# Softmax denominators in attention: GpSimd chains three heads over four key tiles, VectorE reduces the fourth head

## What is computed

```python
c6 = silu(c) @ Wc + bc
sh_msa, sc_msa, g_msa, sh_mlp, sc_mlp, g_mlp = jnp.split(c6, 6, axis=-1)
xm = _modulate(_ln(x), sh_msa, sc_msa)
q = (xm @ Wq + bq).reshape(B, S, NH, DH)
k = (xm @ Wk + bk).reshape(B, S, NH, DH)
v = (xm @ Wv + bv).reshape(B, S, NH, DH)
q = q / DH
w = jnp.einsum('bqhc,bkhc->bhqk', q, k)
w = jax.nn.softmax(w, axis=-1)
y = jnp.einsum('bhqk,bkhc->bqhc', w, v).reshape(B, S, H)
x = x + g_msa[:, None, :] * (y @ Wo + bo)
xm2 = _modulate(_ln(x), sh_mlp, sc_mlp)
h = jax.nn.gelu(xm2 @ W1 + b1, approximate=False)
x = x + g_mlp[:, None, :] * (h @ W2 + b2)
```

## Time and profile before

| | us |
|---|---|
| median of 3 runs | 2990.31 |
| lowest, highest | 2989.18, 2995.33 |
| the profiled execution | 2994.97 |
| its span, first to last instruction | 2993.0 |
| attention in it, first maximum to last sum | about 340 to 2102 |

### The profile page before, as it was taken

One profiled execution on the slowest core, in us unless ns is written; L12 is line 12 of the kernel. 1 busy time (PEld: TensorE's weight loads), 2 busy tenths in 40 slices (PEclk: granted clock), 3 DMA queues, 4 the chain that ended last, 5 costly groups with the idle time before them and its releaser, 6 DMA issues. The chain is left out here.

```text
span 2993.0 us, 40747 instructions
## 1 busy us (share of the span) xinstructions
PE 2886.8 (96%) x14713; PEld 1821.9 (61%) x14713; DVE 2092.1 (70%) x3415; ACT 1343.0 (45%) x2535; POOL 1969.7 (66%) x981
## 2 busy tenths in 40 slices
PE   7999999999999999999999999999699999999998
PEld 5777555455555555555555555553487787777777
DVE  5444687777777777787787777773757757766764
ACT  2222156566666666666666666666111111111111
POOL 1000079889898899898899899887454554545453
PEclk9999789999999999999999999999799999999999
DMA  6444822423414314314323224302201101101000
GB/s 225 176 172 168 204 58 62 95 59 71 103 42 99 88 34 97 86 44 97 79 65 86 68 65 96 77 20 100 88 15 43 42 1 43 43 9 34 29 15 15
DMA packets 152767, 225.19 MB, mean 75 GB/s; under 512 B 31804, under 2 KB 48760, under 8 KB 152568
## 3 DMA queue, kind: packets, MB, share of 16 engines
q1 hardware_dynamic: 123036, 204.81, 25.5%
q10 hardware_dynamic: 29532, 17.79, 2.2%
HBM read 162.30 MB, written 58.97 MB: 74 GB/s over the span
## 5 line engine op out<-in xcount | busy, mean ns | idle before, releaser
L828 DVE TENSOR_REDUCE part_max<-m_bank 128x1 f32<-128x512 f32 x2048 | 1252.4, 680 | 324.7 <-PE m_bank L918 324.6
L809 ACT ACTIVATE probs<-s_bank 128x512 f32<-128x512 f32 x2048 | 1038.7, 625 | 276.8 <-PE s_bank L932 272.8
L932 PE MATMUL s_bank<-qs,ks 97*128 97x512 f32 x2048 | 853.1, 418 | 2.5 <-ACT probs L809 2.4
L721 POOL TENSOR_TENSOR low_sum<-probs 128x1024 f32<-128x1024 f32 x248 | 599.1, 2426 | 188.8 <-ACT probs L809 188.8
L736 POOL TENSOR_TENSOR high_sum<-high_sum,probs 128x1024 f32<-128x1024 f32 x256 | 608.5, 2377 | 45.2 <-ACT probs L809 9.5
L932 PEld LDWEIGHTS s_bank<-qs,ks 97*128 97x128 f32 x2048 | 388.8, 190 | 344.4 <-issue 215.3
L942 PE MATMUL y_bank<-probs,vs 128*32 128x512 f32 x4096 | 504.3, 611 | 0.0
L1308 ACT ACTIVATE h<-up_bank,vecs 128x512 f32<-128x512 f32 x128 | 88.2, 689 | 635.4 <-PE up_bank L1333 635.4
L729 POOL TENSOR_TENSOR high_sum<-probs 128x1024 f32<-128x1024 f32 x128 | 307.7, 2404 | 12.8 <-ACT probs L809 12.8
L942 PEld LDWEIGHTS y_bank<-probs,vs 128*32 128x32 f32 x4096 | 108.3, 110 | 248.6 <-issue 139.1
L918 PE MATMUL m_bank<-space_parts,late_parts 96*128 96x512 f32 x512 | 214.3, 422 | 14.8 <-DVE part_max L828 14.2
(11 more groups left out here) (140 smaller groups left out, 3828.0 us busy)
## 6 DMA issues: line engine op xcount, KB each, us to landing
qs<-q_parts SPq DMA_DIRECT2D x96, 256.0 KB, 5.7
ks<-k_parts SPq DMA_DIRECT2D x96, 256.0 KB, 4.8
q_parts<-qk_out SPq DMA_DIRECT2D x32, 512.0 KB, 3.4
k_parts<-qk_out SPq DMA_DIRECT2D x32, 512.0 KB, 3.7
xb<-in_x SPq DMA_DIRECT2D x12, 1024.0 KB, 7.5
space_parts<-q_parts SPq DMA_DIRECT2D x48, 256.0 KB, 5.0
space_parts<-k_parts SPq DMA_DIRECT2D x48, 256.0 KB, 4.7
late_parts<-k_parts SPq DMA_DIRECT2D x48, 256.0 KB, 4.6
```

The lines of the kernel that those rows point to most:

```text
L721: pool.tensor_tensor(low_sum[:, (2 * c + half) % 4, :, :], probs[:, first % RING, hs, :], probs[:, (first + 1) % RING, hs, :], ALU.add).th ...
L809: act.activation(probs[:, tile % RING, h, :], s_bank[(HPG * tile + h) % 3][:, :], ACT.Exp).then_inc(p_done, 1)
L828: v.tensor_reduce(part_max[:, i % 2, hs, c:c + 1], m_bank[ring.bank["max", i, n]][:, :], AX.X, ALU.max).then_inc(m_taken, 1)
L932: pe.matmul(s_bank[n % 3][:, :], ks[:, h, t * P:(t + 1) * P], qs[i % 2][:, h, :], start=True, stop=True).then_inc(s_done, 1)
```

## The change

- GpSimd no longer makes separate pair sums. For each quad it runs one chain of three additions over **three** heads at once (128x1536) into `chain_sum`. In the last four quads the chain has two heads.
- DVE sums the **fourth** head: `quad` is a `tensor_reduce` over the four key tiles, in two halves of 256 columns. Each half reads 128x1024 values from `probs`, the four tiles innermost, so that consecutive elements lie 8 KB or 16 KB apart in a partition, and writes 128x256. The halves stand between the maxima, two for each quad. In the last four quads DVE sums two heads (`last_quad`), 512 columns at a time.
- All four heads of a quad are then one slot of `chain_sum`, so PE has 4 matmuls for every quad.
- `probs` holds 6 key tiles instead of 5.
- The multiplication of `y_buf` by `inv` goes from DVE to GpSimd, ahead of the chain of the iteration's fourth quad. DVE keeps it only for the last iteration. ACT issues the store of `y` one key tile later.

```diff
-RING = 5
+RING = 6
+CHAIN = HPG - 1
...
-        probs = sb("probs", [P, RING, HPG, TOK])
...
+        probs = sb("probs", [P, RING // 2, 2, HPG, TOK])
...
+        chain_sum = sb("chain_sum", [P, 2, HPG, TOK])
...
+            def chain(c, r):
+                hs = chain_heads(c)
                 pool.wait_ge(p_done, HPG * (4 * c + r) + hs.stop)
...
+                pool.tensor_tensor(chain_sum[:, c % 2, hs, :], first, prob(4 * c + r, hs), ALU.add).then_inc(chain_step, 1)
+
+            def normalise(i):
+                pool.wait_ge(y_taken, i + 1)
+                pool.wait_ge(inv_in, 16 * (i + 1))
+                pool.tensor_tensor(y_buf[:, :], y_buf[:, :], inv[:, :], ALU.mult).then_inc(y_normed, 1)
 
             for c in range(N_QUADS):
...
+                if c >= QPI and c % QPI == QPI - 1:
+                    normalise(c // QPI - 1)
+                for r in (1, 2, 3):
+                    chain(c, r)
...
+            def four_tiles(c, h, cols):
+                first = 4 * c % RING // 2
+                pairs = probs[:, first:first + 2] if first < 2 else probs[:, 0:3:2]
+                return pairs[:, :, :, h, cols].rearrange("p a b n -> p n a b")
+
+            def quad(c, half):
+                if half == 0:
+                    v.wait_ge(p_done, HPG * (4 * c + 4))
+                    if c >= 2:
+                        v.wait_ge(d_done, c - 1)
+                cols = slice(half * TOK // 2, (half + 1) * TOK // 2)
+                v.tensor_reduce(chain_sum[:, c % 2, CHAIN, cols], four_tiles(c, CHAIN, cols), AX.XY, ALU.add).then_inc(quad_ready, 1)
...
+                    if i and n in (14, 17):
+                        quad(QPI * i - 1, (14, 17).index(n))
+                    if n in (30, 33):
+                        quad(QPI * i, (30, 33).index(n))
...
-                    if i and n == NORMALISE_AT:
-                        normalise(i - 1, (inv_in, 16 * i))
+                    if n in (46, 49):
+                        quad(QPI * i + 1, (46, 49).index(n))
+                    if n == 61:
+                        quad(QPI * i + 2, 0)
...
                 as_row(i + 1)
+                quad(QPI * i + 2, 1)
```

More of the change, by code:

```diff
@@ L616, in attend, with prob, chain_heads @@
         wo_in, next_in = sem("wo_in"), sem("next_in")
-        def low_heads(c):
-            return slice(0, 2) if c % 2 == 0 else slice(2, 4)
-        def high_heads(c):
-            return slice(2, 4) if c % 2 == 0 else slice(0, 2)
-        def lows(c, n):
-            return (low_ready, 2 * c + n) if c < LAST_QUAD else (last_low_ready, 2 * (c - LAST_QUAD) + n)
-        def low_slot_free(c, half):
-            return c - 1 + half if c % 2 == 0 else c - 1
+        def prob(tile, heads):
+            slot = tile % RING
+            return probs[:, slot // 2, slot % 2, heads, :]
+        def chain_heads(c):
+            return slice(0, CHAIN if c < LAST_QUAD else 2)
         block = ctx.enter_context(nc.Block())
@@ L713, in _ @@
             pool.memset(ks[STACK:STACK + 1, :, :].bitcast(F32), 1.0).then_inc(ones_row, 1)
-            def low(c, half):
-                first = 4 * c + 2 * half
-                hs = low_heads(c)
-                if c >= 2:
-                    pool.wait_ge(d_done, low_slot_free(c, half))
-                pool.wait_ge(p_done, HPG * (first + 1) + hs.stop)
-                pool.tensor_tensor(low_sum[:, (2 * c + half) % 4, :, :], probs[:, first % RING, hs, :],
-                                   probs[:, (first + 1) % RING, hs, :], ALU.add).then_inc(low_ready, 1)
@@ L808, in _ @@
                             slot_free(tile - RING)
-                        act.activation(probs[:, tile % RING, h, :], s_bank[(HPG * tile + h) % 3][:, :], ACT.Exp).then_inc(p_done, 1)
+                        if tile >= RING:
+                            reduced_free(tile - RING, h)
+                        act.activation(prob(tile, h), s_bank[(HPG * tile + h) % 3][:, :], ACT.Exp).then_inc(p_done, 1)
                     if i:
@@ L891, in _ @@
                         maximum(i + 2, n)
+            for half in range(2):
+                quad(LAST_QUAD - 1, half)
             for q in range(QPI):
-                for half in range(2):
-                    last_low(LAST_QUAD + q, half)
+                for h in range(2, HPG):
+                    last_quad(LAST_QUAD + q, h)
                 if q == 1:
                     invert_small(N_IT - 2)
-                if q == 2:
-                    normalise(N_IT - 2, (inv_in, 16 * (N_IT - 1)))
             for n in range(4):
                 invert_last(n)
-            normalise(N_IT - 1, (inv_ready, 4))
+            normalise_last()
         @block.tensor
@@ L941, in times_v @@
                 for h in range(HPG):
-                    last = pe.matmul(y_bank[h * DH:(h + 1) * DH, :], vs[:, t, h * DH:(h + 1) * DH], probs[:, tile % RING, h, :],
+                    last = pe.matmul(y_bank[h * DH:(h + 1) * DH, :], vs[:, t, h * DH:(h + 1) * DH], prob(tile, h),
                                      start=(t == 0), stop=(t == NKT - 1))
@@ L954, in sums @@
                 first, final = c <= LAST_QUAD, c < LAST_QUAD or c == N_QUADS - 1
[L955 to L970 removed]
+                pe.wait_ge(chain_step, 3 * c + 3)
+                if c < LAST_QUAD:
+                    pe.wait_ge(quad_ready, 2 * (c + 1))
+                else:
+                    pe.wait_ge(last_ready, 2 * (c - LAST_QUAD + 1))
+                for h in range(HPG):
+                    last = add_up(c, h, chain_sum[:, c % 2, h, :], first, final)
                 last.then_inc(d_done, 1)
```

85 lines of the change are left out of this document (31 added, 54 removed).

## The result

| | before | after |
|---|---|---|
| median, us | 2989.74 | 3242.95 |
| lowest, highest | 2988.69, 2995.33 | 3241.48, 3245.19 |
| runs | 4 | 4 |
| the profiled execution, us (span) | 2994.97 (2993.0) | 3241.48 (3239.6) |

The changed kernel takes 1.084 times as long, 95% interval 1.082 to 1.086: 253 us more. I had predicted 175 us more, 3165 us, with a range up to 3240. The direction and most of the mechanism held; the time lies 3 us outside the range and 78 us above the forecast. The step that failed is X, the time by which one half delays the maxima behind it.

What follows compares the result with a forecast made beforehand. PE was taken to set the pace of attention. Terms of -1.72 - 0.99 + 6.33 + 2.03 = +5.65 us an iteration, over 31 iterations +175 us, gave 3165 us, with an 8-in-10 range of 3030 to 3240.

Steps and rivals of the forecast that it cites:

- X: On DVE, the time by which one half delays the maxima behind it: 1.67 us taken, 1.14 at the packed rate.
- What bounds the kernel: In attention PE sets the pace, and nearly every microsecond that PE loses or saves counts in full.
- The sums: On PE, four sum matmuls go, saving 0.86 us twice an iteration: -1.72 us.
- The multiplication: Moved from DVE to POOL, so a late `inv` no longer stops the maxima: -0.99 us an iteration.
- the iteration that I took for clean: Between two negatives, 52.72 us without a late `inv`, against 53.71 us on average.
- GpSimd's load: POOL's chain at 10.7 us a quad is covered; the rival that POOL becomes the bound needs over 14.5, chance 1 in 100.
- the formula: Per iteration: PE waits X - 0.22 and X - 1.01 three times, X in block 6, X - 1.31 in block 7, less 2.71 us.
- My likeliest case for X: X on DVE between 1.5 and 1.9 us, giving 3130 to 3230 us, likeliest 3165; chance 0.60.
- The savings: PE's fewer sums and the multiplication moved off DVE: 2.71 us an iteration, 84 us over 31.
- The clock: Rival: the clock falls at three PE waits an iteration, 1.72 us each, 160 us more, 3325 us; chance 0.09.
- The last iteration: No maxima, saves 2 x 0.86 us, ends behind two longer reductions: +2 us at most, counted as nothing.
- The idle time as rival: DVE's idle time takes up the reductions, only savings remain: 2906 us; faster outcomes (including X at most 0.84 us) chance 0.09.

Runs made afterwards that it cites:

- the kernel with eight columns: The changed kernel, but each half reduces 8 columns instead of 256 and PE takes a GpSimd slot for the fourth head: 2908.64 us.
- near places: The changed kernel, but each half reads two neighbouring heads (2 KB apart) of two neighbouring tiles (8 KB apart): 3244.57 us.
- last quads: The changed kernel with the last four quads treated like all others, three heads chained on GpSimd and the fourth in halves on VectorE: 3237.75 us.
- packed values: The changed kernel, but each half reads 1024 values in a row instead of the fourth head of four key tiles: 3034.98 us.
- two tiles: The changed kernel, but each half reads the fourth head of two key tiles 8 KB apart, alternating, all 512 columns: 3050.07 us.
- pairs: The changed kernel with the fourth head's probabilities of two key tiles interleaved word by word, halves unmoved: 3086.73 us.
- the last split: Against the changed kernel: GpSimd sums the fourth head's tiles 0 and 1, VectorE adds the rest in 256-column pieces, four passes: 2913.23 us, 0.976 of the kernel before.

## Why the prediction was right in kind and wrong in size

**What bounds the kernel**: right. PE set the pace and nearly all that it lost counted. DVE's 306 us of idle time did not take up the reductions where they stood, though there was room for most of them; moved to the ends of the blocks, the same reductions cost 216 us less.

**The sums**, 0.86 us twice an iteration: right. **The multiplication**, put at 0.99 us, was worth 1.2 us by the medians and 1.4 by the traces, since the iteration that I took for clean was not. Both together shortened the iteration by 3.1 us when the halves were next to nothing. GpSimd's load never showed in the changed kernel.

**X is the step that failed.** I took `d_total`'s rate of 1.56 ns a value and got 1.67 us; 1.78 ns and 1.90 us were measured. With X = 1.90 the formula gives 3 x (2X - 1.23) + 2X - 1.31 - 2.71 = 7.49 us an iteration, 7.74 measured. X enters eight times an iteration: 8 x 0.23 x 31 = 57 us of the 78 us missing; another 8 us are the 0.25 us an iteration between 7.49 and 7.74, and about 10 are the last iteration. `d_total`'s instruction has 64 values, of which 100 ns hang on the rate, so an error of 14% in it was a matter of 14 ns. My likeliest case for X ended at 1.9 us, where the measured one lies. The estimate from the 1.73 ns of the Trainium skill (Vector Engine (DVE) Microarchitecture Reference, section 5.2), 3208 us, lay nearer than mine, and the runs' 1.78 ns agrees with the page within 3%.

**How far the formula holds** is seen block by block, against the kernel with eight columns, which has the same order and an iteration of 50.6 us. Blocks 0 to 5 are 7.7 us longer in the changed kernel, and 3 x (2X - 1.23) is 7.71: right. Blocks 6 and 7 are 3.1 us longer where 2X - 1.31 is 2.49, and not in the places that I had named: all of it is in block 6, charged at X alone, and nothing in block 7, charged at X - 1.31 = 0.59. The savings, on the other hand, were 3.1 us and not 2.71. One error takes 0.4 of the other's 0.65 us away, so that the 7.49 us come so near to 7.74 by luck.

**The clock** was a rival at 0.09, and came true in small. Single waits of 1.40 to 1.42 us left the clock up in blocks 0 to 5 of this run. In block 6, where a wait of 1.29 us and one of 0.36 us for the negative follow each other, it fell once in each iteration. PE in block 6, and the starts of blocks 7 and 0:

```profile
1346.73 0.50 PE L947 MATMUL s_bank<-qs,ks 97*128 97x512 f32 x1
...
1351.34 0.49 PE L933 MATMUL m_bank<-space_parts,late_parts 96*128 96x512 f32 x1 [1.29 <-DVE part_max L826]
1352.19 0.31 PE L939 MATMUL m_bank<-ident,neg_max 128*16 128x128 f32 x1 [0.36 <-DVE neg_max L830]
1353.52 2.99 PE L957 MATMUL y_bank<-probs,vs 128*32 128x512 f32 x16
1356.44 0.50 PE L947 MATMUL s_bank<-qs,ks 97*128 97x512 f32 x1
...
1363.07 0.50 PE L947 MATMUL s_bank<-qs,ks 97*128 97x512 f32 x1
```

Block 6 lasts 1356.44 - 1346.73 = 9.71 us and block 7 6.63. The `y_bank` block in it takes 2.99 instead of 1.92 us, at 1.2 GHz for part of it. Meanwhile DVE catches up, which fits that block 7 loses nothing. What the fall costs by itself no run isolates; beyond the formula blocks 6 and 7 lost 0.65 us an iteration together, not 3 x 1.72. What exactly brings the clock down stays open too. With one half of block 6 moved it still fell, elsewhere, and in two other runs with the changed kernel's order (near places, last quads) the first four falls lay in changing blocks before they settled in block 6. No run showed a fall in the steady part where PE's waits for a maximum were 0.3 us or less. With waits of up to 0.7 us there was one fall with packed values, six with two tiles and eleven with pairs, all right behind the negative.

**The last iteration**, costed at nothing with +2 us at most, cost about 10 us. The reductions of 2048 values took 3.79 us and not 3.3, and came in pairs of 7.5 us, once ahead of `d_total` and once ahead of the last sum. The prediction named two reductions of 3.3 us where one addition of 3.0 us stood; that is 3.6 us more, so the bound of 2 us did not follow even from its own numbers.

**The idle time as rival** and its break-even point at X = 0.84 us were not tested closely. At the change's own places there are two runs beside it: with eight columns a half delays the next maximum by about 0.1 us, and the kernel is 79 us faster than before; at X = 1.13 us (packed values) the loss was 47 us, where the formula has 49. The point where gain turns into loss lies between them; no run shows where.

## What to carry over

Before an addition is given to an engine that "has idle time", find where that idle time lies and how many buffers stand between it and the engine that sets the pace: the same reductions cost 216 us less when one stood behind the last maximum of each block. Work that alternates between two places was free of the price that four places paid. That does not make two sums of two and their sum cheap on VectorE: in pieces of 256 columns three such reductions are 0.69 + 0.69 + 0.71 = 2.09 us, an estimate from the rows of the last split, against 1.97 us for one of four places. The split paid because GpSimd had made one of the two sums within its four-head addition. And count an engine's work in what it does at once: a fifth 32-row matmul beside four side by side cost as much as the four.

## What the runs showed of the hardware

- VectorE's reduction read 1024 values in 1206 ns packed, in 1240 ns alternately from two places 8 KB apart, and in 1973 to 1974 ns from four places in turn, whether these lay 8 KB and more apart or two and two 2 KB apart.
- TensorE reading a moving operand with a step of 8 bytes started passes up to 0.49 us apart, against 0.43 us for packed rows.
- Four float32 matmuls into 32 rows each ran together in 0.97 us, up to the start of the next matmul of another kind; one of them alone took 0.95 us by the same measure.
- ScalarE wrote 512 exponentials in 680 ns with a step of 8 bytes and in 623 ns packed, in the same run.
